# A state-space block with an FFN on one core: VectorE adds the last operand of each half's sums, statistics cut in pieces, edge steps re-ordered

## The chip, the cores and the metric

One core of a Trainium2 chip runs the whole program. The metric is the device time of one execution in microseconds. All arithmetic is float32.

## The reference

The input x is 4096 rows of 1024. A selective-scan block (Mamba) and a quantised linear layer follow one another, each with its own layer norm and residual:

```python
H, DIN, N, K, R = 1024, 2048, 16, 4, 64
x, z = split(layernorm(h) @ in_proj_w)                 # each 4096 x DIN
xc = silu(conv_b + sum_k conv_w[:, k] * shifted(x, k)) # causal, 4 taps
ssm_p = xc @ x_proj_w.T                                # 96 columns: dt_r, B, C, each rms-normed
dt = softplus(dt_r @ dt_proj_w.T + dt_bias)
h_t = exp(dt_t * A) * h_(t-1) + dt_t * B_t * x_t       # state of N per channel, over time
y_t = sum_n h_t[n] * C_t[n]
out1 = h + ((y + D * xc) * silu(z)) @ out_proj_w.T
out  = out1 + layernorm(out1) @ dequantised(W).T + bias
```

## The kernel before

Time is cut into 16 chunks of T = 256 rows, the 2048 channels into 8 pairs of two 128-channel tiles. A step is one (chunk c, pair j), 128 steps S = 8 c + j. Beside the scan of its own pair, a step does a share of other chunks' work: the x-projection of chunk c+1, the in-projections of later pairs (x of pair S+9, z of pair S+1), one eighth of the out-projection of chunk c-1 (`out_proj`, four parts, tile g1) and of the FFN of chunk c-2 (`ffn`). Chunk c = 1 has no FFN beside it, c = 0 no out-projection either, c = 15 no in-projection. Two steps of a chunk carry more. In j = 7 the norm of chunk c+2 goes through TensorE (`norm1`: four groups of four transposes into tile gx, each evacuated by ScalarE), and the rms norms of chunk c+1 are made. In j = 0 the second norm does the same (`norm2`, for the FFN of chunk c-2). I call them edge steps.

Each engine has its own order, written out by hand; semaphores join them. Of a step's 16 units (`unit(u)` on ScalarE, `scan(u)` and `product(u)` on VectorE) each takes two of the 16 states of one 128-channel tile:

- ScalarE writes the decays exp(dt*A) into one of four PSUM banks hb (L1061), after saving the last state of the unit that used the bank before (L1057).
- GpSimd makes dbx = dt*x*B for two units at once (L486). VectorE scans in place (L1342) and multiplies by C into hc (L1290).
- GpSimd adds the two halves of hc, which leaves `half` with two operands of 256 columns for each group of two units (L494). `half` has four buffers.
- TensorE adds them into ys[a][:, 0:256] with an identity matrix (L574, `group_sum`, two matmuls for a group). Groups 0 to 3 belong to the pair's tile a = 0, groups 4 to 7 to tile 1. ScalarE has put the skip term D*xc there first (L1080). Groups 6 and 7 are summed at the start of the next step (`late_group`).
- VectorE multiplies ys by the gate silu(z) into ybuf (`y_gate`, L1301): `y_gate(S, 0)` in the middle of the step, `late_y`, which is `y_gate(S-1, 1)`, early in the next. `y_gate` waits for all four groups of its half.

The bank ys[1] also takes the x-projection (L604) and dt_proj (L624), ys[0] the z in-projection (L614), so these wait for the gates. A pair's in-projection lands in gx; ScalarE copies it out and makes the first tap (`x_taps`, L934 to L942), VectorE adds three more (`pair_conv`, six operations at L1238), and the next step's SiLU (L951) makes xcn of it. ScalarE loads tables for the gate's SiLU, for softplus, and back (L1067, L1073, L988, L994).

VectorE takes the norms' statistics in one go: four `bn_stats` (L1218) and two `bn_aggr` (L1223), on xrow in j = 6 and on x2 in j = 7. ScalarE makes the norm's factors (L896 to L902) and rows (L909) from them. The SyncE queue issues nearly all loads in an order of its own: weights one step ahead, each behind a wait for the matmuls that free its tile.

In the rows, an operation of TensorE shows as two records for a float32 matmul, so one group sum is x4 at L574.

## Time and profile before

| | |
|---|---|
| time, median of 3 runs | 4699.61 us (4698.31 to 4702.74) |
| profiled execution: its time | 4697.21 us |
| profiled execution: its span | 4695.4 us |
| TensorE busy, mean granted clock | 4448.9 us, 0.972 of 2.4 GHz |
| VectorE busy | 4160.0 us |
| GpSimd busy | 4039.2 us |
| ScalarE busy | 3542.4 us |

The span runs from the first to the last instruction. A busy share is the time in which at least one instruction of the engine is in work; records of one engine overlap, so the distance between starts is what an operation costs its engine, and its duration is a little more. Most of the span consists of steps that repeat to a hundredth of a microsecond, so single steps can be read for all.

### The profile page before, as it was taken

Reading aid. Unit: us, or ns where it says so; the run is one execution under the profiler, and the core shown is the slowest. Engines: PE = TensorE matmul, PEld = TensorE weight load, DVE = VectorE, ACT = ScalarE, POOL = GpSimd, SP = SyncE. Lnnn points to the kernel's source line nnn. Section 1 sums busy time; section 2 is a strip of 40 time slices with the busy share of each in tenths; the row PEclk is TensorE's granted clock in tenths of the full one; section 3 lists DMA queues with packets and bytes.
Section 4 is the critical chain, followed back from the end, with each engine's and each line's share of the span. In section 5 each row is a group of like instructions: output and inputs, shape, how many; then the busy total and the mean of one; then the engine's idle time right before and its main releaser. Section 6 shows DMA issues by size and latency. Waiting matters only on the chain.

```text
span 4695.4 us, 80181 instructions
## 1 busy us (share of the span) xinstructions
PE 4448.9 (95%) x26656; PEld 4049.0 (86%) x26656; DVE 4160.0 (89%) x5745; ACT 3542.4 (75%) x8848; POOL 4039.2 (86%) x2942
## 2 busy tenths in 40 slices
PE   7788989999999999999999999999999999999889
PEld 6567879989898998989989898998989889898779
DVE  3898989989899998989989899998989989899981
ACT  3777787877778787777877878787787777778760
POOL 0898989989898998989989898998989899899990
PEclk9889999999999999999999999999999999999999
DMA  7324243353434435343353534334353443434232
GB/s 255 130 79 161 99 159 139 114 186 133 173 129 161 145 138 175 124 178 128 123 188 123 177 137 165 137 128 173 138 180 120 145 165 129 165 127 155 90 115 94
DMA packets 160285, 678.56 MB, mean 145 GB/s; under 512 B 21120, under 2 KB 30080, under 8 KB 110720
## 3 DMA queue, kind: packets, MB, share of 16 engines
q1 hardware_dynamic: 141440, 639.88, 39.0%
q10 hardware_dynamic: 18432, 33.56, 1.9%
q8 instruction: 212, 3.47, 0.3%
q14 instruction: 201, 1.65, 0.1%
HBM read 618.32 MB, written 55.05 MB: 143 GB/s over the span
## 4 chain that ended last, share of the span: by engine, by line
PE 59%; DVE 20%; POOL 7%; issue 6%; ACT 5%; DMA 1%; SPq 0%; DVEq 0%; POOLq 0%; ACTq 0%
PE g L767 13%; PE gx L594 13%; PE ys L574 12%; DVE hb L1342 11%; PE ys L614 9%; PE g L689 4%; POOL dbx L486 4%; DVE hc L1290 4%; DVE gx L1238 2%; POOL half L494 2%; PE ys L604 2%; DVE bst L1218 2%; PE gx L581 2%; ACT hb L1061 1%; PE hb L853 1%
## 5 line engine op out<-in xcount | busy, mean ns | idle before, releaser
L1342 DVE TENSOR_TENSOR_SCAN hb<-hb,dbx 128x512 f32<-128x512 f32 x2048 | 2498.0, 1220 | 108.0 <-ACT hb L1061 84.4
L486 POOL TENSOR_TENSOR dbx<-dtx,bb 128x1024 f32<-128x1024 f32 x1024 | 2421.0, 2364 | 60.1 <-DVE hb L1342 34.9
L1061 ACT ACTIVATE hb<-dt,a_neg 128x256 f32<-128x256 f32 x4096 | 1789.5, 468 | 66.3
L494 POOL TENSOR_TENSOR half<-hc 128x512 f32<-128x512 f32 x1024 | 1303.1, 1273 | 135.4 <-DVE hc L1290 120.4
L1290 DVE TENSOR_TENSOR hc<-hb,cb 128x512 f32<-128x512 f32 x2048 | 1378.9, 673 | 0.0
L574 PE MATMUL ys<-half,ident 128*128 128x256 f32 x4096 | 1073.2, 389 | 133.4 <-POOL half L494 119.2
L574 PEld LDWEIGHTS ys<-half,ident 128*128 128x128 f32 x4096 | 757.2, 194 | 254.3 <-POOL half L494 151.3
L767 PEld LDWEIGHTS g<-wo,ybuf 128*128 128x128 f32 x7680 | 954.0, 198 | 20.2 <-issue 1.3
L767 PE MATMUL g<-wo,ybuf 128*128 128x128 f32 x7680 | 966.7, 281 | 0.6 <-issue 0.6
L614 PE MATMUL ys<-xnT,wz 128*128 128x256 f32 x4096 | 928.8, 380 | 1.6 <-DVE ybuf L1301 1.6
L594 PE MATMUL gx<-xnT,wx 128*128 128x256 f32 x3968 | 904.5, 381 | 4.3 <-DMA wx<-in_win 2.6
L1057 ACT COPY hstate<-hb 128x2 f32<-128x2 f32 x2044 | 319.3, 156 | 757.7 <-DVE hc L1290 754.5
L614 PEld LDWEIGHTS ys<-xnT,wz 128*128 128x128 f32 x4096 | 770.6, 191 | 103.1 <-DVE ybuf L1301 2.8
L594 PEld LDWEIGHTS gx<-xnT,wx 128*128 128x128 f32 x3968 | 756.9, 192 | 108.5 <-DMA wx<-in_win 3.0
L689 PEld LDWEIGHTS g<-wf,x2nT 128*128 128x128 f32 x3552 | 414.1, 192 | 5.7
L689 PE MATMUL g<-wf,x2nT 128*128 128x128 f32 x3552 | 414.5, 275 | 0.0
L1301 DVE TENSOR_TENSOR ybuf<-ys,gate 128x256 f32<-128x256 f32 x256 | 107.0, 418 | 237.8 <-PE ys L574 237.6
L1238 DVE SCALAR_TENSOR_TENSOR gx<-xpre,convw,gx 128x256 f32<-128x256 f32 x744 | 302.0, 482 | 13.8 <-ACT gx L942 13.8
L512 POOL TENSOR_TENSOR dtx<-dt,xcs 128x2 f32<-128x2 f32 x128 | 25.3, 198 | 282.7 <-ACT dt L992 176.8
L604 PE MATMUL ys<-xprojw,xcn 128*128 128x96 f32 x1024 | 152.0, 298 | 26.6 <-ACT xcn L951 23.5
L604 PEld LDWEIGHTS ys<-xprojw,xcn 128*128 128x128 f32 x1024 | 143.2, 215 | 33.9 <-issue 21.5
L1067 ACT ACT_TABLE_LOAD x128 | 164.2, 1283 | 2.3
(105 smaller groups left out, 2766.1 us busy)
## 6 DMA issues: line engine op xcount, KB each, us to landing
wz<-in_win SPq DMA_DIRECT2D x128, 1024.0 KB, 4.8
wx<-in_win SPq DMA_DIRECT2D x124, 1024.0 KB, 4.8
wo<-in_wout SPq DMA_DIRECT2D x123, 1024.0 KB, 4.9
wf<-wf_scratch SPq DMA_DIRECT2D x113, 512.0 KB, 3.2
xc_scratch<-xcn ACTq DMA_DIRECT2D x128, 256.0 KB, 2.1
xcs<-xc_scratch SPq DMA_DIRECT2D x128, 256.0 KB, 5.0
bb<-bc_scratch SPq DMA_DIRECT2D x64, 512.0 KB, 7.5
cb<-bc_scratch SPq DMA_DIRECT2D x64, 512.0 KB, 6.7
```

The lines of the kernel that those rows point to most:

```text
L486: nc.gpsimd.tensor_tensor(dbx[:, k % 2, :].rearrange("p (n t) -> p n t", n=NQ), dtx[:, S % 2, a, :].unsqueeze(1).to_broadcast([P, NQ, T]), ...
L494: nc.gpsimd.tensor_tensor(half[:, k % 4, :], hc[:, k % 2, 0:HALF], hc[:, k % 2, HALF:GW], ALU.add).then_inc(halves, 1)
L574: mm = nc.tensor.matmul(ys[a][:, 0:T], ident[:], half[:, k % 4, i * T:(i + 1) * T], start=False, stop=(q == NQ - 1 and i == 1), skip_group ...
L594: mm = nc.tensor.matmul(pair_bank(q)[:, a * T:(a + 1) * T], pair_weights(q)[:, kk, a * P:(a + 1) * P], xnT[:, chunk % 2, kk, :], start=(kk ...
L604: mm = nc.tensor.matmul(ys[1][:, tt * E:(tt + 1) * E], xcn[:, a * T + tt * P:a * T + (tt + 1) * P], xprojw[:, 2 * (q % PAIRS) + a, :], sta ...
L614: mm = nc.tensor.matmul(ys[0][:, a * T:(a + 1) * T], wz[:, kk, a * P:(a + 1) * P], xnT[:, q // PAIRS % 2, kk, :], start=(kk == 0), stop=(k ...
L689: mm = nc.tensor.matmul(g1[:, tt * P:(tt + 1) * P], x2nT[:, kk, tt * P:(tt + 1) * P], wf[:, kk, :], start=(kk == 0), stop=(kk == KH - 1))
L767: mm = nc.tensor.matmul(g1[:, tt * P:(tt + 1) * P], ybuf[:, (1 - st.parity) * PAIRS + kt // 2, (kt % 2) * T + tt * P:(kt % 2) * T + (tt + ...
L1061: ins = nc.scalar.activation(h[:, m * T:(m + 1) * T], dt[:, j % 2, a, :], ACT.Exp, scale=a_neg[:, ds((2 * j + a) * N + 2 * v + m, 1)])
L1238: nc.vector.scalar_tensor_tensor(bank[:, a * T:(a + 1) * T], xpre[:, a, tap:tap + T], convw[:, ds((2 * jq + a) * KC + tap, 1)], bank[:, a ...
L1290: nc.vector.tensor_tensor(hc[:, k % 2, w * UW:(w + 1) * UW], hb[u % 4][:], cb[:, n:n + 2, :].rearrange("p n t -> p (n t)"), ALU.mult).then ...
L1342: nc.vector.tensor_tensor_scan(h[:], h[:], dbx[:, k % 2, w * UW:(w + 1) * UW], 0.0, ALU.mult, ALU.add).then_inc(scans, 1)
```

## The change

- Of groups 3 and 7 TensorE adds only the first operand of `half`; VectorE adds the second to ys itself (`last_sum`) and signals `summed`, for which `y_gate` waits. One scan lies between the two. In the second half's case this is `late_sum`, before scan(3), and the gate comes behind scan(3). In j = 7 the sum of the first half stands behind scan(12).
- GpSimd waits for the gate of the former user before it writes the `half` buffer of groups 3 and 7.
- TensorE's order: out-projection parts 2 and 3 move behind dt_proj, part 1 ahead of the x-projection. In the edge steps transposes are spread between other work; in j = 0 out-projection comes first and the in-projection of x last.
- ScalarE: the norm's start and rows move (`norm1` into j = 6 between units 8 and 11; the rows of `norm2` behind units 6 and 7 of j = 0, its evacuations behind units 8 to 11). `x_taps` of edge steps moves behind unit 14.
- VectorE: each `bn_stats` becomes a piece of its own at the end of a step: xrow's in j = 1 to 4 with the aggregate in j = 5, x2's in j = 5, 6 and twice in j = 7. Taps of edge steps move behind product(13).

```diff
@@ -491,6 +492,9 @@
             def group_sum(S, k):
                 pool.wait_ge(hcs, after(UNITS * S + 2 * k + 2))
                 pool.wait_ge(sum_mm, after(8 * S + k - 3))
+                if k % NQ == NQ - 1:
+                    pool.wait_ge(y_ready, after(2 * S + k // NQ))
                 nc.gpsimd.tensor_tensor(half[:, k % 4, :], hc[:, k % 2, 0:HALF], hc[:, k % 2, HALF:GW],
                                         ALU.add).then_inc(halves, 1)
 
@@ -570,9 +574,10 @@
 
                 a, q = divmod(k, NQ)
                 pe.wait_ge(halves, after(8 * SG + k + 1))
-                for i in range(2):
+                for i in range(1 if q == NQ - 1 else 2):
                     mm = nc.tensor.matmul(ys[a][:, 0:T], ident[:], half[:, k % 4, i * T:(i + 1) * T],
-                                          start=False, stop=(q == NQ - 1 and i == 1), skip_group_check=True)
+                                          start=False, stop=(q == NQ - 1), skip_group_check=True)
                 mm.then_inc(sum_mm, 1)
 
             def transposes(rows, i, bank, done):
@@ -788,33 +793,55 @@
                     ffn()
                     late_group(6)
                     late_group(7)
-                    if first and st.ffn or last and st.norm1:
-                        norm2(0)
+                    if last and st.norm1:
                         norm1(0)
                         x_proj()
+                        out_proj(0)
+                        norm1(1)
+                        group(0)
+                        norm1(2)
+                        out_proj(1)
+                        norm1(3)
+                        x_in_proj(0)
+                        group(1)
+                        ss_transpose()
+                        x_in_proj(1)
+                        group(2)
+                        group(3)
+                        dt_proj()
+                        out_proj(2)
+                        out_proj(3)
+                    elif first and st.ffn:
+                        out_proj(0)
+                        out_proj(1)
+                        x_proj()
+                        group(0)
+                        out_proj(2)
+                        norm2(0)
+                        out_proj(3)
+                        group(1)
                         norm2(1)
-                        norm1(1)
-                        out_proj(0)
+                        group(2)
+                        dt_proj()
                         norm2(2)
-                        norm1(2)
-                        group(0)
+                        group(3)
                         norm2(3)
-                        norm1(3)
+                        x_in_proj(0)
+                        x_in_proj(1)
                     else:
                         out_proj(0)
+                        out_proj(1)
                         x_proj()
-                    out_proj(1)
-                    if not (first and st.ffn or last and st.norm1):
                         group(0)
-                    x_in_proj(0)
-                    group(1)
-                    ss_transpose()
-                    x_in_proj(1)
-                    group(2)
-                    out_proj(2)
-                    group(3)
-                    dt_proj()
-                    out_proj(3)
+                        x_in_proj(0)
+                        group(1)
+                        ss_transpose()
+                        x_in_proj(1)
+                        group(2)
+                        group(3)
+                        dt_proj()
+                        out_proj(2)
+                        out_proj(3)
                     z_in_proj(1)
                     group(4)
                     z_in_proj(0)
...
@@ -1147,47 +1174,51 @@
                         if last and st.inproj:
                             chunk_ss_out(c + 1)
 
+                    edge = first and st.ffn or last and st.norm1
                     unit(0)
                     unit(1)
+                    unit(2)
                     norm2_start()
-                    norm2_row(0)
-                    unit(2)
-                    norm2_row(1)
                     unit(3)
                     if S == 0:
                         pair_taps(PAIRS)
                     silus()
-                    norm2(0)
-                    norm1(0)
                     unit(4)
                     first_skip_term()
-                    norm2(1)
+                    norm1(0)
+                    unit(5)
                     norm1(1)
-                    unit(5)
-                    norm2(2)
+                    unit(6)
+                    norm2_row(0)
                     norm1(2)
-                    unit(6)
-                    norm2(3)
+                    unit(7)
+                    norm2_row(1)
                     norm1(3)
-                    unit(7)
                     rms_square()
                     unit(8)
+                    norm2(0)
                     rms_apply()
+                    norm1_start()
                     unit(9)
+                    norm2(1)
+                    norm1_row(0)
                     unit(10)
+                    norm2(2)
+                    norm1_row(1)
                     unit(11)
+                    norm2(3)
                     ss_out()
                     unit(12)
-                    x_taps()
+                    if not edge:
+                        x_taps()
                     dt_softplus()
                     unit(13)
                     first_decays_out()
                     second_skip_term()
                     unit(14)
-                    norm1_start()
-                    norm1_row(0)
+                    if edge:
+                        x_taps()
                     unit(15)
-                    norm1_row(1)
 
                 steps(c, step)
 
...
         def _(dve):
-            def stats(rows, bst, mv, mid, done, n):
-                for tt in range(TT):
-                    for h in range(2):
-                        ins = nc.vector.bn_stats(bst[:, tt, 6 * h:6 * h + 6], rows(tt, h))
-                ins.then_inc(mid, 1)
-                dve.wait_ge(mid, after(n))
-                dve.sem_inc(aggr_go, 1)
+            def aggregate(bst, mv, mid, done, n):
+                dve.wait_ge(mid, after(4 * n))
                 for tt in range(TT):
                     ins = nc.vector.bn_aggr(mv[:, tt, :], bst[:, tt, :])
                 ins.then_inc(done, 1)
 
+            def norm1_piece(chunk, i):
+                tt, h = divmod(i, 2)
+                dve.wait_ge(xrow_in, landed(chunk + 1))
+                dve.wait_ge(l1_stats, after(chunk))
+                nc.vector.bn_stats(bst1[:, tt, 6 * h:6 * h + 6], xrow[:, tt, h * 512:(h + 1) * 512]).then_inc(l1_dve, 1)
+            def norm1_aggregate(chunk):
+                aggregate(bst1, mv1, l1_dve, l1_stats, chunk + 1)
             def norm1_stats(chunk):
-                dve.wait_ge(xrow_in, landed(chunk + 1))
-                stats(lambda tt, h: xrow[:, tt, h * 512:(h + 1) * 512], bst1, mv1, l1_dve, l1_stats, chunk + 1)
+                for i in range(4):
+                    norm1_piece(chunk, i)
+                norm1_aggregate(chunk)
 
             def pair_conv(q):
 
@@ -1272,11 +1309,15 @@
                 nc.vector.tensor_tensor(blk, bank[:, 0:TT * P].rearrange("p (t h) -> p t h", t=TT), blk, ALU.add
                                         ).then_inc(done, 1)
 
-            def norm2_stats_of(chunk):
-                dve.wait_ge(o_add, after(PAIRS * (chunk + 1)))
-                rows = x2[:, chunk % 2, :]
-                stats(lambda tt, h: rows[:, tt * H + h * 512:tt * H + (h + 1) * 512], bst2, mv2, l2_dve,
-                      l2_stats, chunk + 1)
+            def norm2_piece(chunk, tt, h):
+                dve.wait_ge(o_add, after(PAIRS * chunk + 4 * (h + 1)))
+                dve.wait_ge(l2_stats, after(chunk))
+                nc.vector.bn_stats(bst2[:, tt, 6 * h:6 * h + 6],
+                                   x2_rows(chunk % 2)[:, tt, h * 512:(h + 1) * 512]).then_inc(l2_dve, 1)
+            def norm2_aggregate(chunk):
+                aggregate(bst2, mv2, l2_dve, l2_stats, chunk + 1)
 
             def times_c(SU, u):
 
@@ -1291,10 +1332,18 @@
                                         cb[:, n:n + 2, :].rearrange("p n t -> p (n t)"), ALU.mult
                                         ).then_inc(hcs, 1)
 
+            def last_sum(SP, a):
+                k = NQ * (a + 1) - 1
+                dve.wait_ge(sum_mm, after(8 * SP + k + 1))
+                dve.wait_ge(halves, after(8 * SP + k + 1))
+                nc.vector.tensor_tensor(ys[a][:, 0:T], ys[a][:, 0:T], half[:, k % 4, T:HALF], ALU.add
+                                        ).then_inc(summed, 1)
             def y_gate(SP, a):
 
                 chunk, jp = divmod(SP, PAIRS)
-                dve.wait_ge(sum_mm, after(8 * SP + NQ * (a + 1)))
+                dve.wait_ge(summed, after(2 * SP + a + 1))
                 dve.wait_ge(sz_act, after(SP + 1))
 
                 dve.wait_ge(o_mm, after(PAIRS * (chunk - 1)))
@@ -1351,6 +1400,10 @@
                         if was.scan and not (first and c == 0):
                             times_c(S - 1, UNITS - 1)
 
+                    def late_sum():
+                        if was.scan and not (first and c == 0):
+                            last_sum(S - 1, 1)
                     def late_y():
                         if was.scan and not (first and c == 0):
                             y_gate(S - 1, 1)
@@ -1385,10 +1438,20 @@
                         if last and st.inproj:
                             chunk_sums(c + 1)
 
-                    def norm2_stats():
-                        if last and st.outproj:
-                            norm2_stats_of(c - 1)
+                    def norm_stats():
+                        if st.norm1 and 1 <= j <= 4:
+                            norm1_piece(c + 2, j - 1)
+                        if st.norm1 and j == 5:
+                            norm1_aggregate(c + 2)
+                        if st.outproj and j in (5, 6):
+                            norm2_piece(c - 1, j - 5, 0)
+                        if st.outproj and last:
+                            norm2_piece(c - 1, 0, 1)
+                            norm2_piece(c - 1, 1, 1)
+                            norm2_aggregate(c - 1)
+                    edge = first and st.ffn or last and st.norm1
                     scan(0)
                     late_product()
                     scan(1)
@@ -1398,8 +1461,9 @@
                     add_ffn()
                     scan(2)
                     product(1)
+                    late_sum()
+                    scan(3)
                     late_y()
-                    scan(3)
                     product(2)
                     scan(4)
                     product(3)
@@ -1415,22 +1479,30 @@
                     product(7)
                     scan(9)
                     product(8)
-                    if pre and st.norm1:
-                        norm1_stats(c + 2)
                     scan(10)
                     product(9)
-                    y_gate(S, 0)
+                    if not (last and st.norm1):
+                        last_sum(S, 0)
                     scan(11)
+                    if not (last and st.norm1):
+                        y_gate(S, 0)
                     product(10)
                     scan(12)
+                    if last and st.norm1:
+                        last_sum(S, 0)
                     product(11)
-                    taps()
+                    if last and st.norm1:
+                        y_gate(S, 0)
+                    if not edge:
+                        taps()
                     scan(13)
                     product(12)
                     add_out()
-                    norm2_stats()
+                    norm_stats()
                     scan(14)
                     product(13)
+                    if edge:
+                        taps()
                     scan(15)
                     product(14)
```

## Rows read from the trace of the kernel before

**Rows 1.** Busy time of each engine over the whole span (page, part 1).

```profile
PE 4448.9 (95%) x26656; PEld 4049.0 (86%) x26656; DVE 4160.0 (89%) x5745; ACT 3542.4 (75%) x8848; POOL 4039.2 (86%) x2942
```

**Rows 2.** Stretches: length, busy time by engine, clock, DMA; from gate to gate.

```profile
1939.46:1972.66 33.20, 33.20 (x206) 30.61 (x205) 31.60 (x44) 26.04 (x65) 32.07 (x24) 1.00 0.38 130
...
2005.86:2040.29 34.43, 33.95 (x208) 30.83 (x206) 34.12 (x50) 29.20 (x72) 32.15 (x24) 1.00 0.39 138
2040.29:2081.55 41.26, 36.33 (x224) 32.27 (x222) 36.69 (x55) 33.49 (x87) 32.74 (x26) 1.00 0.47 167
2081.55:2119.72 38.17, 37.03 (x218) 34.37 (x219) 29.82 (x41) 28.05 (x69) 30.87 (x24) 0.91 0.61 227
...
1801.70:2081.55 279.85, 273.30 (x1666) 250.52 (x1666) 258.63 (x359) 220.91 (x553) 252.50 (x184) 0.99 0.42 149
...
539.00:573.35 34.35, 31.82 (x173) 28.27 (x173) 31.28 (x43) 26.03 (x66) 30.83 (x23) 0.95 0.31 110
```

**Rows 3.** TensorE's order of time in an ordinary step: start, duration, what.

```profile
1986.33 1.03 PE L574 MATMUL ys<-half,ident 128*128 128x256 f32 x4
1987.19 1.95 PE L767 MATMUL g<-wo,ybuf 128*128 128x128 f32 x16
1988.97 1.03 PE L574 MATMUL ys<-half,ident 128*128 128x256 f32 x4
```

**Rows 4.** VectorE in the same step; in brackets its idle time before.

```profile
1990.04 0.42 DVE L1301 TENSOR_TENSOR ybuf<-ys,gate 128x256 f32<-128x256 f32 x1 [1.44 <-PE ys L574]
1990.38 1.22 DVE L1342 TENSOR_TENSOR_SCAN hb<-hb,dbx 128x512 f32<-128x512 f32 x1
1991.51 0.67 DVE L1290 TENSOR_TENSOR hc<-hb,cb 128x512 f32<-128x512 f32 x1
1992.10 1.22 DVE L1342 TENSOR_TENSOR_SCAN hb<-hb,dbx 128x512 f32<-128x512 f32 x1
...
1993.82 2.44 DVE L1238 SCALAR_TENSOR_TENSOR gx<-xpre,convw,gx 128x256 f32<-128x256 f32 x6
1996.16 1.22 DVE L1342 TENSOR_TENSOR_SCAN hb<-hb,dbx 128x512 f32<-128x512 f32 x1
```

**Rows 5.** VectorE in j = 6: the four pieces on xrow.

```profile
2020.00 2.46 DVE L1218 BATCH_NORM_STATS2 bst<-xrow 128x6 f32<-128x512 f32 x4
```

**Rows 6.** TensorE in the edge steps j = 7 and j = 0.

```profile
2039.40 1.13 PE L574 MATMUL ys<-half,ident 128*128 128x256 f32 x4 [0.47 <-POOL half L494]
2041.43 0.66 PE L581 MATMUL gx<-ident,xrow 128*128 128x128 f32 x4 [0.90 <-ACT xcn L951]
...
2078.98 1.13 PE L574 MATMUL ys<-half,ident 128*128 128x256 f32 x4 [2.42 <-POOL half L494]
2082.69 1.11 PE L581 MATMUL gx<-ident,xrow 128*128 128x128 f32 x4 [2.58 <-ACT xcn L951]
...
2086.10 2.92 PE L767 MATMUL g<-wo,ybuf 128*128 128x128 f32 x16
```

**Rows 7.** VectorE in the edge steps: scan 0 of j = 7, and gates.

```profile
2036.08 1.22 DVE L1342 TENSOR_TENSOR_SCAN hb<-hb,dbx 128x512 f32<-128x512 f32 x1
...
2060.87 0.42 DVE L1301 TENSOR_TENSOR ybuf<-ys,gate 128x256 f32<-128x256 f32 x1 [3.74 <-PE ys L574]
...
2103.90 0.42 DVE L1301 TENSOR_TENSOR ybuf<-ys,gate 128x256 f32<-128x256 f32 x1 [4.06 <-PE ys L574]
```

**Rows 8.** Order of time in chunk c = 1, without FFN.

```profile
538.10 1.73 PE L574 MATMUL ys<-half,ident 128*128 128x256 f32 x4 [2.40 <-POOL half L494]
...
557.52 0.43 DVE L1301 TENSOR_TENSOR ybuf<-ys,gate 128x256 f32<-128x256 f32 x1 [2.58 <-PE ys L574]
```

**Rows 9.** ScalarE: softplus's table load, the next unit, a norm row.

```profile
1989.84 1.28 ACT L988 ACT_TABLE_LOAD   x1
...
1993.10 0.16 ACT L1057 COPY hstate<-hb 128x2 f32<-128x2 f32 x1
...
2075.93 1.24 ACT L909 ACTIVATE xrow<-x,nmr,rstd 128x1024 f32<-128x1024 f32 x1
```

13 lines of the change are left out of this document (9 added, 4 removed).

## The prediction

> **What bounds the kernel now.** I read the totals first, then the stretches step by step, then each engine's order of time inside one ordinary step, the two long steps, and last a step of the chunk that has no FFN. In the totals TensorE leads with 4448.9 us of 4695.4, VectorE has 4160.0 [rows 1]. An average can't say which of them ends a step, so the second view cuts the span from one gate SiLU to the next, about one step each. An ordinary step (j = 1 to 5 of chunks 2 to 13) takes 33.20 us and TensorE is busy for all 33.20 of it; VectorE works 31.60 and stands still 1.60. Three of the eight steps are longer: 34.43 (j = 6), 41.26 (j = 7) and 38.17 (j = 0). A chunk is 5 x 33.20 + 34.43 + 41.26 + 38.17 = 279.86 us, in which TensorE has 273.30 and VectorE 258.63 of work [rows 2]. So ordinary steps are TensorE's, and the chunk loses 6.5 us of TensorE's time in its edge steps, plus what a slower clock costs (0.91 in the j = 0 stretch).
>
> Inside an ordinary step the fourth view shows where VectorE's idle time is: 1.44 us in front of the gate multiply, which waits for TensorE's fourth group sum; TensorE runs 1.78 us of out-projection before that group sum [rows 3, 4]. In the chunk without FFN (c = 1) a step takes 34.35 us though neither engine has more than 31.82 of work [rows 2]: TensorE waits 2.40 us for GpSimd's half 7, and 2.58 us later in the step VectorE waits for TensorE's group 3 [rows 8]. That is a loop: half 7, TensorE's order up to group 3, the gate, VectorE's second half of the step, half 7 again.
>
> **The sums.** The change takes one of two identity matmuls out of groups 3 and 7. A group is four records (two matmuls, two passes) that take 1986.33 to 1987.19, 0.86 us, so each removal is 0.43 and a step loses 0.86: 33.20 becomes 32.34 on TensorE [rows 3]. VectorE gets two additions of 128x256 with one operand and the result in PSUM, which the trace doesn't have. Nearest below is the gate multiply (PSUM read, 128x256): 1990.04 to the next start 1990.38, 0.34. Nearest above is a convolution tap (PSUM read and written, three operands): six in 1993.82 to 1996.16, 0.39 each [rows 4]. It differs from either in one thing, so I take the middle, 0.36, and keep 0.33 and 0.42 (the whole duration of one such multiply, nothing overlapped) as ends. Two are 0.72 a step, 96 steps with their neighbours: each 0.03 is worth 0.5 us a chunk. The Trainium skill speaks against the change here: "VectorE: DVE Perf Modes", section "The DRAIN you can't avoid", has the next VectorE operation start only when the pipe is empty, and its rules advise fewer operations. By that rule an addition costs its full 0.42, and the sum would be some 12 us worse. The rows show the next start 0.34 after a 0.42 us multiply began, so here they overlap.
>
> **Statistics.** The four pieces on the xrow tile take 2.46 us in j = 6, 0.6 each [rows 5]; they go one each to j = 1 to 4, the aggregate (about 0.26) to j = 5. Of the four pieces on x2, one goes to j = 5, one to j = 6, two and the aggregate stay in j = 7. Nothing of this is saved, only moved, and VectorE is now what it lands on. So an ordinary step on VectorE is 31.60 + 0.72 + 0.60 = 32.92, above TensorE's 32.34: **VectorE becomes the bound of j = 1 to 4 and 6**, at 32.92; j = 5 gets 31.60 + 0.72 + 0.60 + 0.26 = 33.18. The 0.16 us left of VectorE's idle time (scan 4, behind ScalarE's table loads) is covered by the late sum put in front of it.
>
> Does a wait come on top? New order on TensorE from the second half of late group 7: out-projection parts 0 and 1 (3.57), x-projection 0.87, group 0, in-projection (3.45), group 1, in-projection, group 2, half a group: 0.43 + 3.57 + 0.87 + 3 x 0.86 + 2 x 3.45 + 0.43 = 14.8 after half 7. Late group 7's matmul, which waited for half 7, starts at 2039.40, 3.3 us after scan 0 at 2036.08 [rows 6, 7]. VectorE reaches last_sum after 10 units of 1.72 (scan 1.13, product 0.59 [rows 4]) and some 3 us of adds, 20.2 after scan 0. TensorE is there at 3.3 + 14.8 = 18.1, or 18.8 when its x-projection waits for the late gate (which now lies behind scan 3, 7.4 after scan 0) and group 3 waits for half 3. Slack 1.4 us. The other way, the second z-projection wants y_gate at 22.0 and comes at 23.3. Both covers hold, so I add no wait. GpSimd's new wait for y_ready before sums 3 and 7 is long fulfilled (the gate it names is over 10 us earlier); behind it in GpSimd's queue stands the next dbx, so it would cost one for one if it weren't. GpSimd itself has 30.85 or 32.07 of work by parity, the latter within 0.9 of the step.
>
> **The four edge steps** (j = 6, 7, 0, 1) take 34.43 + 41.26 + 38.17 + 33.20 = 147.06 us now, VectorE's work in them is 34.12 + 36.69 + 29.82 + 31.60 = 132.23, so it waits 14.8, of which 3.74 and 4.06 in front of the gate multiply [rows 2, 7]. Work after: + 8 x 0.36, less four pieces and an aggregate that leave (2.66) = 132.4. The waits after, walked through by the orders:
> - j = 6: the norm's start and its two rows (some 1.2 us each on ScalarE) now lie between units 8 and 11, where ScalarE's unit takes 1.0 against VectorE's 1.72: no wait.
> - j = 7: TensorE's transposes 0 still wait for the xcn SiLU, 2.0 us after late group 7 begins [rows 6], the x-projection for the late gate, and the evacuations follow at units 4 to 7. Transposes 3 come some 3.3 us later than now, because two out-projection parts (1.79 each) precede them. So ScalarE's evacuations delay scan 6 by 0.55, the squares come 1.15 late for VectorE's sums, 0.15 at scan 9. The old 3.74 in front of the gate goes, as last_sum now stands after scan 12. Instead softplus is late: it waits for dt_proj, and from its table load to the next unit is 3.26 us, 1989.84 to 1993.10 [rows 9]; the taps no longer cover this in front of scan 13, 1.45. Together 3.3.
> - j = 0: out-projection 0 waits for the late gate (its chunk's last ybuf), so TensorE idles about 2.7 after late group 7 and everything behind is late: VectorE's add of the x-projection 0.6, scans 10 and 11 behind evacuations 0.8, and scan 13 behind softplus with no taps in front, 2.0. Together 3.4.
> - j = 1: both in-projections of j = 0 have moved behind the transposes, so TensorE comes to j = 1's FFN 2.5 us after VectorE wants it. And as now (idle 2.42 and 2.58, then an out-projection part of 2.92 instead of 1.78 [rows 6]) I expect TensorE's clock at 1.2 GHz after the 2.7 us gap, some 1.5 more: 4.0.
>
> Sum 132.4 + 3.3 + 3.4 + 4.0 = 143.1, against 147.06: -4.0. With j = 2 to 5 (3 x 32.92 + 33.18 = 131.9 against 132.8) a chunk gets 275.0, -4.9. The walk is good to 4 us a chunk either way: it stacks some twenty small offsets.
>
> **The rest.** From j = 7 of c = 1 to j = 6 of c = 13 are 12 such chunks: -59. In c = 1 the loop of [rows 8] is cut by 1.79 + 0.43 + 0.43 before group 3, more than VectorE's slack, so VectorE bounds it: 31.28 + 0.72 + 0.60 = 32.6 against 34.35, seven steps, -12. The last edge pair and c = 14 (no xrow pieces, 32.3 to 32.9 a step): -7. In c = 0 TensorE has time to spare, VectorE only gets longer; bounds 0 and 8 x 0.72 = 6, taken 3. c = 15, the tail and the start: 0, one addition of 0.4 in the tail.
> Profiled execution 4697.21 (span 4695.4 and 1.8 around it) - 59 - 12 - 7 + 3 = 4622; the median of the runs lies 2.4 above it, so **4625 us**, -1.6%.
>
> **Rivals.**
> (a) *The clock stays up and the edges close.* If TensorE's gap in j = 0 leaves the clock at 2.4 GHz and ScalarE's evacuations are early enough, a chunk loses another 3 us: 4625 - 13 x 3 = 4586. For it: a 0.90 us gap left the clock up; against it: 2.42 and 2.58 didn't [rows 6], nor 2.40 in c = 1 [rows 8].
> (b) *The clock falls in j = 7 too.* There the gaps before and after transposes 0 add up to 3.0 us. The out-projection part then takes 2.92 for 1.78, and its follower transposes feed ScalarE, scan 6 and the squares: 1.5 to 2 us a chunk, 4625 + 13 x 1.8 = 4648. The Trainium skill, "TensorE: Matmul & The Clock Gate", Part 1, holds half rate for the default that only activity lifts, which is this rival's side; the rows above show a fall in j = 0 and none in j = 7.
> (c) *The addition is dear or VectorE's edge waits stay as large as now* (14.8 instead of 10.7 in the four steps): the chunk gains 0.8, 4625 + 12 x 4.1 = 4674.
> (d) *Slower.* Place: last_sum in ordinary steps. If group 3 comes after VectorE (for instance since TensorE, delayed by the late gate behind scan 3, never catches up), the loop of c = 1 exists in all chunks. The gain of an ordinary step is 0.28, so from a wait of 0.3 us the step has none, and with the 1.44 us of today a step is 34.4: 12 x 6 x 1.44 = 104 more, 4729. Against it is the slack of 1.4 worked out above.
> (e) *No change*: gains at the edges eaten by a wait of 0.7 to 1 us in each step, or 6 us more at each edge pair: 4700.
>
> **How the numbers follow.** Forecast 0.45 (its own range 4600 to 4648), (a) 0.17, (b) 0.12, (c) 0.10, (d) 0.10, (e) 0.06. The range 4572 to 4692 takes in (a), (b), (c) and part of what lies between, and leaves out (d), (e) and edges better still. 0.2% (9 us) is what a measurement of this kernel can tell from none. Faster 0.83, same 0.06, slower 0.11.
>
> **What would show it.** Ordinary steps of 32.9 us with VectorE busy all through and TensorE idle some 0.5 us, at group 3 or the x-projection; group sums with 3584 instead of 4096 records; no wait in front of the gate multiply; additions with a pitch near 0.36. Steps of 32.3 would mean that the pieces cost nothing, steps above 33.2 that (d) holds. In the edge steps: waits of scan 13 for ScalarE, an add of the FFN late in j = 1, and the four steps together near 143. The prediction is wrong if the edges, whose walk carries the most terms, close better or worse than 4 us a chunk.

## The result and the profile after

The changed kernel takes 4659.73 us (median of 4 runs, 4655.04 to 4661.43), against 4699.67 (4698.31 to 4702.74) for the kernel before: ratio 0.9912, 95% interval 0.9897 to 0.9928, so 0.9% faster. Forecast were 4625, in a range of 4572 to 4692. The sign was right, its size was not: 40 us came where 75 were forecast. The time lies in the stated range, but outside the forecast's own 4600 to 4648, between rivals (b), 4648, and (c), 4674.

The totals of the page after:

```profile
PE 4375.0 (94%) x26144; PEld 3937.5 (85%) x26144; DVE 4235.7 (91%) x6001; ACT 3533.8 (76%) x8848; POOL 4030.4 (86%) x2942
...
DVE 44%; PE 26%; issue 17%; POOL 7%; DMA 2%; ACT 2%; SPq 1%; DVEq 0%; POOLq 0%; ACTq 0%
...
L579 PE MATMUL ys<-half,ident 128*128 128x256 f32 x3584 | 970.8, 394 | 115.4 <-POOL half L498 110.3
```

512 matmul records fewer than before and 256 operations of VectorE more [rows 1]; the chain that ended last is now VectorE's. The group sums are the 3584 records foretold.

Stretches from gate to gate (length, busy time and count of PE, PEld, DVE, ACT, POOL, then clock, DMA share, GB/s): an ordinary step, the edge steps j = 7, j = 0 and j = 1, a whole chunk, and one step of the last chunk.

```profile
1341.58:1374.24 32.66, 32.66 (x201) 29.66 (x201) 32.66 (x47) 25.97 (x65) 30.74 (x23) 1.00 0.39 131
1472.37:1512.43 40.06, 36.92 (x218) 33.11 (x218) 34.75 (x52) 31.17 (x85) 30.57 (x23) 0.96 0.42 145
1512.43:1549.85 37.42, 33.90 (x197) 30.52 (x198) 31.65 (x44) 30.02 (x71) 33.78 (x27) 0.95 0.66 246
1549.85:1585.30 35.45, 35.45 (x223) 32.33 (x222) 33.40 (x48) 26.14 (x65) 30.13 (x23) 1.00 0.42 148
1196.06:1472.37 276.31, 269.52 (x1635) 244.18 (x1635) 263.20 (x375) 220.19 (x553) 251.76 (x184) 0.99 0.43 151
...
4319.79:4355.85 36.06, 29.89 (x174) 26.32 (x173) 29.83 (x38) 23.91 (x60) 31.93 (x24) 0.86 0.26 88
```

An ordinary step went from 33.20 [rows 2] to 32.66, and VectorE is busy for all of it. So is TensorE: the 0.5 us of idle time that I had named as a sign did not show, and which of the two ends the step is settled below, by doubling the addition. The addition itself, in the order of time of VectorE:

```profile
1342.26 0.67 DVE L1331 TENSOR_TENSOR hc<-hb,cb 128x512 f32<-128x512 f32 x1
1342.85 0.42 DVE L1340 TENSOR_TENSOR ys<-ys,half 128x256 f32<-128x256 f32 x1
1343.18 1.22 DVE L1391 TENSOR_TENSOR_SCAN hb<-hb,dbx 128x512 f32<-128x512 f32 x1
```

0.42 us long, 0.33 to the next start (the pitch, what it costs VectorE), and no wait before it; nor is one left before the gate multiply, where [rows 4] have 1.44.

Cut at the starts of the gate SiLU, the two traces differ as follows (us; "foretold" is the prediction's term):

| stretch | before | after | difference | foretold |
|---|---|---|---|---|
| start to j = 7 of c = 0 | 362.98 | 364.33 | +1.35 | +3 |
| on to j = 7 of c = 1 | 279.14 | 273.47 | -5.7 | -12 |
| 12 chunks, to j = 7 of c = 13 | 3357.37 | 3305.70 | -51.7 | -59 |
| on to j = 7 of c = 14 | 278.66 | 276.09 | -2.6 | -7 |
| on to j = 7 of c = 15 | 261.21 | 275.43 | **+14.2** | 0 |
| from there to the end | 156.01 | 164.58 | **+8.6** | 0 |
| span | 4695.4 | 4659.6 | -35.8 | -75 |

So 23 of the 39 us missing (in spans) lie in the last chunk and the tail, where I had foretold no change. Waits of VectorE in the last chunk, then TensorE's order of time in one of its steps:

```profile
4288.37 0.42 DVE L1309 TENSOR_TENSOR x<-g,x 128x256 f32<-128x256 f32 x1 [0.54 <-PE g L694]
...
4323.65 0.42 DVE L1309 TENSOR_TENSOR x<-g,x 128x256 f32<-128x256 f32 x1 [4.57 <-PE g L694]
...
4358.29 0.42 DVE L1309 TENSOR_TENSOR x<-g,x 128x256 f32<-128x256 f32 x1 [3.14 <-PE g L694]
```

```profile
4289.63 3.73 PE L772 MATMUL g<-wo,ybuf 128*128 128x128 f32 x32
4293.20 1.03 PE L579 MATMUL ys<-half,ident 128*128 128x256 f32 x4
4296.18 1.13 PE L579 MATMUL ys<-half,ident 128*128 128x256 f32 x4 [1.95 <-POOL half L498]
4300.02 2.08 PE L579 MATMUL ys<-half,ident 128*128 128x256 f32 x4 [2.71 <-POOL half L498]
4303.55 1.22 PE L579 MATMUL ys<-half,ident 128*128 128x256 f32 x2 [1.46 <-POOL half L498]
4304.57 1.91 PE L629 MATMUL ys<-ssmT,dtw 65*128 65x256 f32 x4
4306.27 5.07 PE L772 MATMUL g<-wo,ybuf 128*128 128x128 f32 x32
4311.18 3.62 PE L619 MATMUL ys<-xnT,wz 128*128 128x256 f32 x16
```

The same step in the kernel before: groups 2 and 3 with part 2 of the out-projection between them, then VectorE's wait:

```profile
4358.15 2.07 PE L574 MATMUL ys<-half,ident 128*128 128x256 f32 x4 [2.71 <-POOL half L494]
4360.01 2.62 PE L767 MATMUL g<-wo,ybuf 128*128 128x128 f32 x16
4362.47 1.03 PE L574 MATMUL ys<-half,ident 128*128 128x256 f32 x4
...
4378.46 0.42 DVE L1272 TENSOR_TENSOR x<-g,x 128x256 f32<-128x256 f32 x1 [1.48 <-PE g L689]
```

The last chunk has no in-projection and no x-projection. Without them nothing stands between group sums 0 to 2, in either kernel: TensorE idles up to 2.71 us for GpSimd's halves and its clock falls (sums of 1.03 us take 2.07 or 2.08). What is new is ahead of group 3. There part 2 of the out-projection used to fill the wait for the last half; now TensorE idles 1.46 us more, and part 2 comes behind group 3 with part 3, partly at the lower clock: 5.07 us for the two. The z-projections, the groups and the next step's FFN follow back to back, and VectorE waits up to 4.57 us for that FFN, where it waited 1.48 to 1.50.

In the tail one wait stands out, on TensorE:

```profile
4535.75 6.40 PE L865 MATMUL g<-wf,x2nT 128*128 128x128 f32 x32 [6.61 <-DMA wf<-wf_scratch]
```

### The profile page after: what moved, and what is told of

It reads as the page before. It is cut to its first block, busy times and chain, and to the rows that moved or that the text cites. A ratio compares the mean times of both kernels' runs of the same rounds, so it can differ in the third digit from the quotient of the medians.

```text
span 4659.6 us, 79778 instructions
## 1 busy us (share of the span) xinstructions
PE 4375.0 (94%) x26144; PEld 3937.5 (85%) x26144; DVE 4235.7 (91%) x6001; ACT 3533.8 (76%) x8848; POOL 4030.4 (86%) x2942
## 4 chain that ended last, share of the span: by engine, by line
DVE 44%; PE 26%; issue 17%; POOL 7%; DMA 2%; ACT 2%; SPq 1%; DVEq 0%; POOLq 0%; ACTq 0%
DVE hb L1391 23%; DVE hc L1331 12%; PE gx L599 6%; PE g L772 5%; POOL dbx L487 4%; PE ys L579 4%; DVE gx L1275 4%; PE ys L619 4%; POOL half L498 2%; PE g L694 2%; DVE ybuf L1350 1%; PE hb L880 1%; DVE ys L1340 1%; DVE x L1309 1%; PE ys L609 1%
## 5 line engine op out<-in xcount | busy, mean ns | idle before, releaser
L579 PE MATMUL ys<-half,ident 128*128 128x256 f32 x3584 | 970.8, 394 | 115.4 <-POOL half L498 110.3
L772 PEld LDWEIGHTS g<-wo,ybuf 128*128 128x128 f32 x7680 | 939.3, 200 | 50.4 <-issue 38.0
L772 PE MATMUL g<-wo,ybuf 128*128 128x128 f32 x7680 | 944.3, 283 | 31.8 <-issue 31.8
L619 PE MATMUL ys<-xnT,wz 128*128 128x256 f32 x4096 | 928.8, 380 | 11.5 <-DVE ybuf L1350 11.5
L579 PEld LDWEIGHTS ys<-half,ident 128*128 128x128 f32 x3584 | 650.4, 193 | 268.0 <-POOL half L498 191.0
L1309 DVE TENSOR_TENSOR x<-g,x 128x256 f32<-128x256 f32 x240 | 98.4, 410 | 102.2 <-PE g L694 63.1
```

The costliest lines, as they stand in the source:

```text
L579: mm = nc.tensor.matmul(ys[a][:, 0:T], ident[:], half[:, k % 4, i * T:(i + 1) * T], start=False, stop=(q == NQ - 1), skip_group_check=True)
L619: mm = nc.tensor.matmul(ys[0][:, a * T:(a + 1) * T], wz[:, kk, a * P:(a + 1) * P], xnT[:, q // PAIRS % 2, kk, :], start=(kk == 0), stop=(k ...
L772: mm = nc.tensor.matmul(g1[:, tt * P:(tt + 1) * P], ybuf[:, (1 - st.parity) * PAIRS + kt // 2, (kt % 2) * T + tt * P:(kt % 2) * T + (tt + ...
```

## The experiments

**Is it the order in the last chunk?** Only there, one part of the out-projection goes back ahead of group 3:

```
+elif not st.inproj:
+    out_proj(0); out_proj(1)
+    group(0); group(1); group(2)
+    out_proj(2)
+    group(3)
+    dt_proj(); out_proj(3)
 else:
     ...
```

> The changed kernel; only in chunk 15 (no in-projection) TensorE does out-projection part 2 ahead of group 3 again, as the kernel before. In the changed kernel chunk 15 lost 14 us against before and the tail 8.5 us. Theory A (order): TensorE has nothing to do while it waits for groups 0 to 3 in this chunk, so an out-projection part put behind group 3 is added to the path group 3, z-projection, FFN, VectorE's add of the FFN. With it back ahead of group 3, 1.8 us of path go per step: 7 steps, 10 to 14 us, and part of the tail comes back since the loads of the tail are queued behind the last out-projection and start 2 us earlier: 4640 to 4650. Theory B (sums): VectorE's two additions a step (0.65 us x 8) and the scan between addition and gate lengthen the step there; the order does nothing: 4655 to 4662.

Measured: 4628.54 us (4618.85 to 4636.67), ratio 0.9846 (0.9831 to 0.9861), below the 4640 to 4650 expected. The last chunk takes 261.91 instead of 275.43, the tail 156.5 instead of 164.6: both losses are gone with this one edit, which shows the order as their cause. VectorE's wait in the step shown is as before, though TensorE still idles 2.70 us and its clock still falls:

```profile
4278.31 2.08 PE L579 MATMUL ys<-half,ident 128*128 128x256 f32 x4 [2.70 <-POOL half L498]
...
4298.97 0.42 DVE L1319 TENSOR_TENSOR x<-g,x 128x256 f32<-128x256 f32 x1 [1.50 <-PE g L694]
```

The remaining 9 us or so lie in chunks that the edit doesn't touch (see the clock below; a second series of this kernel gave 4634.1).

The other side, **the kernel before with the new ordinary order alone** (no additions, statistics and edges as before):

```
 else:
     out_proj(0)
+    out_proj(1)
     x_proj()
     group(0)
     ...
-    out_proj(2)
     group(3)
     dt_proj()
+    out_proj(2)
     out_proj(3)
```

> The kernel before with TensorE's new order of an ordinary step alone (out-projection part 1 ahead of the x-projection, parts 2 and 3 behind dt_proj); sums, statistics, edge steps as before. Theory A: ordinary steps with FFN stay TensorE's, 33.2, as no work leaves it; chunk 1 gains about 1.5 us a step (group 3 comes 1.8 earlier in the loop half 7 to gate), -10; chunk 15 loses by the order about as much as the changed kernel does, +12 to +20 with the tail: 4695 to 4712. Theory B (chunk 15's loss comes from the sums): 4685 to 4692.

Measured: 4713.7 us (4705.58 to 4716.8), ratio 1.0026 (1.0017 to 1.0036). This is just above the 4695 to 4712 expected. A middle chunk stays at 279.9; c = 1 gains 11.5, the last chunk loses 14.9 and the tail 7.8. The order by itself wins nothing where TensorE is the bound, and loses at the end.

**The additions alone**, in the kernel before, with its order: one identity matmul less in groups 3 and 7, `last_sum` on VectorE, a scan between it and the gate, GpSimd's new wait.

```
-for i in range(2):
+for i in range(1 if q == NQ - 1 else 2):
     ...
+def last_sum(SP, a): ...
```

> The kernel before with the sums alone (one matmul less in groups 3 and 7, the additions on VectorE, a scan between addition and gate); orders of TensorE and ScalarE, statistics and taps as before. Theory A: TensorE's order up to group 3 with an out-projection part ahead of it is the longer path: late gate 7.4 us after scan 0, then 14.3 us of TensorE up to group 3, so last_sum waits 1.5 us and an ordinary step takes 33.6 against 33.2: +0.4 x 80 steps, edges the same: 4720 to 4745, slower. Theory B: TensorE's work bounds the step, 0.86 us less of it shows: ordinary steps 32.3 to 32.5, 4620 to 4640.

Measured: 4797.18 us (4794.83 to 4799.44), ratio 1.0206 (1.019 to 1.0221): slower, as theory A has it, but by 97 us, not by 20 to 45. An ordinary step takes 34.04 (33.6 was expected), and neither engine fills it:

```profile
1624.69:1658.73 34.04, 32.65 (x202) 29.85 (x202) 32.16 (x46) 26.04 (x65) 32.07 (x24) 1.00 0.37 126
...
1593.84 1.13 PE L607 MATMUL ys<-xprojw,xcn 128*128 128x96 f32 x8 [1.39 <-DVE ybuf L1312]
...
1608.54 0.43 DVE L1302 TENSOR_TENSOR ys<-ys,half 128x256 f32<-128x256 f32 x1 [1.88 <-PE ys L577]
```

The first row is the step; the others lie in the step before it. TensorE waits 1.39 us for the late gate (`late_y`, now behind scan 3), and 15 us later VectorE waits 1.88 for group 3. This is my rival (d), TensorE delayed by the late gate: from there its order up to group 3, the addition, VectorE's second half, the next late gate. With an out-projection part ahead of group 3 this loop sets the length. The chunk's two long steps grow too: j = 7 takes 42.2 or 45.3 in turn, where it took 41.26. Each of the two edits alone loses. That they gain together no run shows by itself, but the ordinary steps do: 33.20 before, 33.20 with the order alone, 34.04 with the additions alone, and 32.50 to 32.65 with both and no piece of the statistics (the next kernel).

**The statistics in one go**, the changed kernel otherwise:

```
-if st.norm1 and 1 <= j <= 4:
-    norm1_piece(c + 2, j - 1)
-if st.norm1 and j == 5:
-    norm1_aggregate(c + 2)
+if st.norm1 and j == 5:
+    norm1_stats(c + 2)
 ...
```

The four pieces on x2 are then all in j = 7.

> The changed kernel with the statistics in one go: the four pieces and the aggregate on xrow at j = 5, the four on x2 at j = 7. Theory A (VectorE is the bound of ordinary steps): j = 1 to 4 fall from 32.66 to TensorE's 32.34, j = 5 rises by 1.8 less 0.6 = 1.2, j = 6 falls by 0.3, j = 7 rises by 1.2: +0.8 a chunk, 4665 to 4680. Theory B (TensorE is the bound of ordinary steps at 32.66 of busy time): j = 1 to 4 stay at 32.66, then +2.4 a chunk: 4685 to 4695.

Measured: 4695.4 us (4690.65 to 4696.45), ratio 0.9989 (0.9979 to 0.9998); a chunk takes 276.9 or 279.4 in turn, mean 278.2 against 275.5. The 4665 to 4680 of theory A did not come. Ordinary steps are only 0.1 shorter without their piece:

```profile
1588.00:1620.50 32.50, 32.50 (x202) 29.69 (x200) 32.03 (x46) 26.05 (x66) 31.95 (x24) 1.00 0.39 132
...
1620.09 0.42 DVE L1309 TENSOR_TENSOR x<-g,x 128x256 f32<-128x256 f32 x1 [0.47 <-PE g L694]
```

TensorE is busy throughout and VectorE now waits 0.32 to 0.47 for it in each such step: the piece of 0.6 filled idle time of VectorE. In return j = 5 grows from 32.80 to 35.3. Taken out of the changed kernel, the pieces cost 2.7 us a chunk, 33 of the 52 us that the twelve chunks gain. Not all of that is their work: 0.7 of the 2.7 lies in j = 0, which has no piece in either kernel, and whose granted clock is 0.95 or 0.91 here and 1.00 in five of the twelve chunks of the changed kernel.

**Is VectorE the bound of an ordinary step?** This and the next kernels start from the one with the last chunk mended. Here each last addition runs twice, first into a tile that nobody reads.

```
+nc.vector.tensor_tensor(spare[:], ys[a][:, 0:T], half[:, k % 4, T:HALF], ALU.add)
 nc.vector.tensor_tensor(ys[a][:, 0:T], ys[a][:, 0:T], half[:, k % 4, T:HALF], ALU.add
                         ).then_inc(summed, 1)
```

> As the kernel beside it, and VectorE does each half's last addition twice, the first time into a tile that nobody reads. Two more additions of 0.33 us pitch in each of 128 steps. Theory A (an ordinary step is bound by VectorE's own sequence): an ordinary step goes from 32.66 to 33.3, at most 33.5, the whole run by 128 x 0.66 = 84 us, to about 4710. Theory B (TensorE, busy 32.5 us of such a step, bounds it as well and VectorE has slack): the step stays at 32.66 to 32.9 and the run below 4660.

Measured: 4739.13 us (4735.79 to 4742.54), ratio 1.0083 (1.0068 to 1.0098).

```profile
1318.73:1352.06 33.33, 32.94 (x202) 29.75 (x201) 33.33 (x49) 26.07 (x66) 32.01 (x24) 1.00 0.37 128
...
1286.67 0.41 DVE L1351 TENSOR_TENSOR spare<-ys,half 128x256 f32<-128x256 f32 x1
1287.00 0.42 DVE L1352 TENSOR_TENSOR ys<-ys,half 128x256 f32<-128x256 f32 x1
```

The step grows by 0.67, twice the pitch of 0.33, to the full: VectorE's sequence bounds it. The whole run grew by 105 us, more than the 84 expected: j = 7 went from at most 40.1 to 41.7 and j = 0 from at most 37.5 to 38.6, so the edges cost extra. The trace shows by what: j = 7 has a granted clock of 1.00 in one of the twelve chunks, where it is only 0.33 longer than the base's shortest, and 0.92 in the other eleven (0.96 in the base's long ones).

```profile
1209.16:1247.93 38.77, 34.67 (x214) 31.09 (x214) 35.40 (x55) 31.17 (x86) 29.86 (x24) 1.00 0.47 162
1485.51:1527.28 41.77, 38.05 (x219) 34.39 (x217) 35.39 (x54) 31.15 (x86) 30.68 (x23) 0.92 0.41 142
```

Why the clock is lower there was not tried.

**What is the edge order worth?** The same base a second time, beside it with the edge steps j = 7 and j = 0 in the order of before on TensorE, ScalarE and VectorE (sums, pieces and ordinary order kept).

```
-if last and st.norm1:
-    norm1(0)
-    x_proj()
-    out_proj(0)
+if first and st.ffn or last and st.norm1:
+    norm2(0)
+    norm1(0)
+    x_proj()
+    norm2(1)
     ...
```

> The kernel of the run before that moved one part of the out-projection of the last chunk back ahead of group 3, a second time, so that the three other kernels of this call have it beside them on the same chip. Theory A (the edge steps have two lengths, j=7 of 38.4 us with TensorE's granted clock at 1.00 and of 40.1 us with it lowered, and which of them a chunk gets differs between executions): a median between 4618 and 4645, with single runs more than 5 us apart. Theory B (the version gives 4628 each time and the scatter is chance of one chip): 4626 to 4631 with runs within 4 us.

> As the kernel beside it (after, with the last chunk's out-projection mended), but the two edge steps j=7 and j=0 keep the order of before on TensorE, ScalarE and VectorE; the sums, the pieces of the statistics and the ordinary order stay. Theory A (my prediction: the edge re-ordering takes waits of VectorE out of j=7, j=0 and j=1, about 3 to 4 us of a chunk): j=7 and j=0 together 2 to 4 us longer, 4655 to 4680. Theory B (the gain of a chunk is that of the ordinary steps and of the statistics, and the re-ordering of the edges only moves their waits): within 10 us of the kernel beside it.

Measured: the base 4634.1 us (4622.24 to 4635.96), ratio 0.9853 (0.9837 to 0.987); with the old edges 4649.8 (4647.1 to 4651.3), ratio 0.9892 (0.9877 to 0.9907). The two series of the base, 4618.85 to 4636.67 and 4622.24 to 4635.96, scatter alike. The edge order is worth 16 us, about a third of the 3 to 4 us a chunk that I gave it, and between my two theories. With the old edges nearly all chunks are alike, j = 7 42.56, j = 1 32.66 and a chunk 276.2 to 276.8; the new order shortens j = 7 and lengthens j = 1 to 35.50, where VectorE waits for the FFN. With the new ones j = 7 has two lengths in one and the same execution of the base, 40.06 and 38.44:

```profile
3390.49:3428.93 38.44, 35.31 (x218) 31.49 (x218) 34.76 (x52) 31.16 (x86) 30.85 (x23) 1.00 0.44 154
...
3938.47:3978.53 40.06, 37.17 (x219) 33.35 (x220) 34.75 (x52) 31.17 (x85) 30.95 (x23) 0.96 0.44 148
```

TensorE at the start of either, the short one first:

```profile
3391.63 0.66 PE L586 MATMUL gx<-ident,xrow 128*128 128x128 f32 x4 [0.47 <-ACT xcn L988]
3393.68 1.13 PE L609 MATMUL ys<-xprojw,xcn 128*128 128x96 f32 x8 [1.39 <-DVE ybuf L1360]
3394.65 1.98 PE L772 MATMUL g<-wo,ybuf 128*128 128x128 f32 x16
...
3939.61 0.66 PE L586 MATMUL gx<-ident,xrow 128*128 128x128 f32 x4 [0.46 <-ACT xcn L988]
3941.66 1.61 PE L609 MATMUL ys<-xprojw,xcn 128*128 128x96 f32 x8 [1.39 <-DVE ybuf L1360]
3943.07 3.16 PE L772 MATMUL g<-wo,ybuf 128*128 128x128 f32 x16
```

The same order with the same gaps, 0.47 and 1.39 us; behind them TensorE goes on at 2.4 GHz in one chunk (granted clock 1.00 in the stretch) and falls to 1.2 for a while in the other (0.96). The next transposes start 1.6 us later, and j = 7 is 1.6 us longer: ScalarE's evacuation, scan 6 and all behind them move along. A chunk of the base is 273.1 to 273.3 where the clock stays up in j = 7 and in most of j = 0, and up to 276.5 where it falls in both. The new edge order pays only where the clock stays up: 276.5 is what the old order takes.

**Filling the gap in j = 7**: the first out-projection part ahead of the x-projection, since it doesn't need the late gate that the x-projection waits 1.39 us for.

```
 norm1(0)
+out_proj(0)
 x_proj()
-out_proj(0)
```

> As the kernel beside it, but in the edge step j=7 the first part of the out-projection stands ahead of the x-projection, in the time in which TensorE waits 1.39 us for the late gate. Theory A (that idle time on TensorE is what lowers its granted clock in the long form of j=7): the clock stays at 1.00 through j=7 in nearly all chunks, j=7 is 38.4 us or less, and the run 4612 to 4625. Theory B (the x-projection comes later by a part of the out-projection, and the norm chain behind it holds VectorE at scan 6): j=7 40 us or more and the run 4635 to 4655.

Measured: 4609.38 us (4607.31 to 4617.0), ratio 0.9809 (0.9795 to 0.9824), a little below the range expected. j = 7 is 37.10 in every chunk from c = 3 to 13, one length only, at a granted clock of 1.00 in each: the gap was what lowered the clock there. j = 0 still mostly takes 37.1, and TensorE shows why:

```profile
1455.78:1492.88 37.10, 35.34 (x218) 31.47 (x218) 34.64 (x52) 31.08 (x86) 30.45 (x23) 1.00 0.46 159
...
1493.40 0.70 PE L579 MATMUL ys<-half,ident 128*128 128x256 f32 x2 [1.08 <-POOL half L498]
1496.12 5.44 PE L772 MATMUL g<-wo,ybuf 128*128 128x128 f32 x32 [2.02 <-issue]
```

The first row is j = 7. In j = 0 TensorE idles 1.08 and 2.02 us, then parts 0 and 1 take 5.44 instead of 3.73. The second gap is a wait in the code: part 0 waits for the last pair's gated half, which only part 3 reads.

**Filling that gap too**, with the change of j = 7 and without it:

```
 if part == 0:
     ...
-    if first:
-        pe.wait_ge(y_ready, after(2 * c * PAIRS))
     ...
+if part == 3 and first:
+    pe.wait_ge(y_ready, after(2 * c * PAIRS))
```

> The kernel that put the out-projection's first part ahead of the x-projection in j=7, and in j=0 the out-projection waits for the last pair's gated half (the late gate) only ahead of its part 3, the only part that reads it, in place of part 0. TensorE's idle 2.02 us in front of the out-projection of j=0 goes. Theory A (the late gate leaves TensorE idle, its granted clock falls to 0.95 in j=0, and the evacuations on ScalarE, scan 13 and the FFN addition of j=1 come late because of both): clock 1.00 in j=0, j=0 37.1 to 35.4 or less, j=1 35.5 to 34.5 or less, chunk 273.1 to 270 or 271.5, the run 4575 to 4595. Theory B (the waits of j=0 and j=1 are set by ScalarE's norm rows and the order, not by TensorE's start; the waiting time moves to the transposes): j=0 and j=1 together at most 0.7 us shorter, the run 4600 to 4612.

> The wait of j=0 moved as in the kernel beside it, but j=7 keeps the order of after (x-projection ahead of the out-projection's first part); the last chunk is mended in both. Theory A: j=7 in two lengths, 38.4 or 40.1 us, as in the kernels with that order so far, and j=0 shorter than 37.4 wherever the clock stays up; a run 12 to 25 us above the kernel beside it and with runs more than 5 us apart. Theory B (what sets the clock in j=7 is how j=0 to j=6 of the chunk went): with j=0 cured j=7 is 38.4 throughout, and the run within 15 us of the kernel beside it with runs less than 4 us apart.

Measured: both gaps 4586.73 us (4584.21 to 4588.77), ratio 0.9756 (0.9743 to 0.9769); j = 0 alone 4612.43 (4606.78 to 4624.08), ratio 0.9815 (0.9802 to 0.9829). In the first:

```profile
1489.97 0.70 PE L579 MATMUL ys<-half,ident 128*128 128x256 f32 x2 [0.86 <-POOL half L498]
1490.51 3.73 PE L772 MATMUL g<-wo,ybuf 128*128 128x128 f32 x32
...
1489.66:1525.67 36.01, 32.76 (x197) 29.23 (x198) 31.79 (x44) 30.01 (x71) 33.66 (x27) 1.00 0.69 253
...
1527.71 0.42 DVE L1319 TENSOR_TENSOR x<-g,x 128x256 f32<-128x256 f32 x1 [2.74 <-PE g L694]
```

The chunk's mean goes 275.2 (base), 273.6 (j = 7 filled), 271.9 (both filled), and the runs with both lie within 5 us of each other. With both filled the granted clock of j = 0 is 1.00 in eleven of twelve chunks. With j = 0 filled alone the mean is 274.0, j = 7 keeps its two lengths, 38.4 and 40.1, and the runs lie 17 us apart: its own gap decides. The kernel with both filled beats both kernels of the change, by 115 and 73 us. I was wrong about j = 1: its wait of 2.74 us for the FFN stays. TensorE works from the in-projection of j = 0 to that FFN without a gap; that in-projection waits for the last of ScalarE's evacuations, which the transposes of the norm set.

## Why the prediction was right in sign and short in size

- *TensorE's bound.* Right: the matmuls left, and VectorE took over an ordinary step. I had TensorE at 32.34; with the statistics taken out of the way it shows 32.50 to 32.65. Both engines are within 0.2 us of each other, so little more is to be had from either alone.
- *The addition.* I took 0.36 out of 0.33 to 0.42; it is 0.33, and the doubled addition shows 0.33 again. A nearer row than the two that I used stood in the trace before, an addition of 128x256 that reads PSUM:

```profile
1931.48 0.41 DVE L1272 TENSOR_TENSOR x<-g,x 128x256 f32<-128x256 f32 x1
1931.81 1.22 DVE L1342 TENSOR_TENSOR_SCAN hb<-hb,dbx 128x512 f32<-128x512 f32 x1
```

The full 0.42 that I drew from the Trainium skill ("VectorE: DVE Perf Modes", "The DRAIN you can't avoid") took only half of what that section says: its first paragraph ends with the remark that a next operation which is not held starts earlier. The pitch of 0.33 agrees with that remark and not with the 0.42.
- *Ordinary step.* Foretold 32.92 and 33.18 (j = 5), measured 32.66 and 32.80. 0.06 is the addition. The rest is how I read "busy": it counts each operation to its end, also where the next starts before that end; ahead of a wait that overlap is absent, so 31.60 was not the sum of the pitches; 32.66 less two additions and a piece leaves 31.40. Worth 1.1 us a chunk in j = 2 to 5, in my favour.
- *Slack of last_sum.* Right, and needed: no wait in ordinary steps, and with the old order 1.88 us of one.
- *Statistics.* "Only moved, nothing saved" was right in work but underrated: taking them out costs 33 of the 52 us that twelve chunks gain, because they moved from steps that had no room to steps where VectorE would have waited for TensorE.
- *The edges.* The four steps j = 6, 7, 0, 1: 143.1 foretold. With the clock up in j = 7 and j = 0 they are 32.7 + 38.4 + 35.5 + 35.5 = 142.1, with it down in both 32.7 + 40.1 + 37.4 + 35.5 = 145.7; 144.7 in the mean of the changed kernel. My walk had the clock down after j = 0's gap only; that it falls in j = 7 too was rival (b), given 0.12, and it holds in 7 of 12 chunks of the profiled run. The waits of VectorE, in the chunk of the rows shown and against my numbers: scan 6 2.44 (0.55), squares 0.97 (1.15), scan 13 of j = 7 1.71 (1.45), x-projection's add 1.75 (0.6), scan 13 of j = 0 1.97 (2.0), the FFN's in j = 1 2.74 (4.0). What was mis-sized hangs for the most part on the clock. With the clock up in j = 7, scan 6 waits 0.82, near my 0.55; and the FFN's wait is 2.74 also with the clock up in j = 0 (the kernel with both gaps filled), so the 1.5 that I had added there for the clock didn't come. That the sum came within 1.6 us is partly luck: these errors cancel.
- *c = 1.* -12 foretold, -5.7 measured. Multiplying by seven steps failed: only j = 1 to 5 had 34.3 before, and they gave 7.3; j = 0 and j = 6 gave 1.0, and j = 7 of c = 0, which the stretch includes, lost 2.6.
- *"c = 15, the tail and the start: 0".* The step that failed, worth 23 us. I had worked out what is behind half 7 and ahead of group 3 with the x-projection and the in-projections in it, and did not do so for the chunk that has none. In that chunk part 2 of the out-projection filled a wait; behind group 3 it lengthens the path to the FFN, which was not in the sum at all: +14.2, and +8.6 in the tail. There the out-projection's last parts again come late and at a lower clock, and TensorE waits 6.61 us for weights where it waits 2.00 with the order mended and 0.72 in the kernel before; that the loss goes with the order is shown, which of those two carries it is only argued.

Without the last chunk and the tail the forecast would have missed by 16 us of span: 7 in the twelve chunks, 6 in c = 1, 4 in c = 14, and 1.6 the other way in c = 0. The 7 are in the main a balance: 1.1 us a chunk too pessimistic in j = 2 to 5, 1.6 too hopeful at the edges.

## What to carry to other kernels

When an order written by hand is changed, walk through it once for each kind of iteration, above all those where some of the calls do nothing: work moved behind a wait is only free where something else still stands in front of it. When two engines are within a few tenths of each other, count what each edit leaves on both, and test pairs of edits together, since each may lose alone. And look for a wait set earlier than the first instruction that reads the data: here, moved from part 0 to part 3, together with one reordered call, it was worth about as much as the whole change (0.9853 to 0.9756, against 1 to 0.9912).

## What the runs showed of the hardware

- One and the same gap can cost nothing or 1.6 us. In one execution of the kernel with the last chunk mended, behind 0.47 and 1.39 us of idle time in j = 7, TensorE went on at 2.4 GHz in some chunks (x-projection 1.13 us) and at 1.2 in others (1.61). A kernel with such gaps scatters: 17.8 us between runs of one kernel, against 4.6 with the gaps filled. Longer gaps don't scatter: behind 2.42 and 2.58 us [rows 6] the kernel before has a granted clock of 0.91 or 0.92 in j = 0 of every middle chunk, and its runs lie 4.4 us apart. In the kernel with the statistics in one go the outcome alternates chunk by chunk, 1.00 and 0.96 in j = 7. The Trainium skill, "TensorE: Matmul & The Clock Gate", Part 1, says that what watches TensorE's activity runs on by itself and doesn't start anew with the kernel; two outcomes of one gap would fit this, but no run here shows it.
- An addition of 128x256 with operand and result in PSUM costs VectorE the same 0.33 us pitch as one that writes SBUF (the spare one, 1286.67 to 1287.00).
